# Attention outputs in two blocks of eight heads instead of four blocks of four, in a four-layer transformer kernel

## The reference, cut to what matters

```python
h = layernorm(x) * (1 + scale1) + shift1
q, k, v = h @ Wq + bq, h @ Wk + bk, h @ Wv + bv        # 16 heads of 16
p = softmax(q @ k.T * HEAD_DIM ** -0.5)                # per head, 256 x 256
x = x + gate1 * ((p @ v) @ Wo + bo)
h = layernorm(x) * (1 + scale2) + shift2
x = x + gate2 * (gelu(h @ W1 + b1) @ W2 + b2)          # blocks 0, 1, 3
# block 2 instead: h1 = attention + x;  x = layernorm(h1) * gamma + beta + h1
```

## Time and profile before

| what | us |
|---|---|
| median of 3 runs | 1201.23 (1201.06 to 1201.85) |
| profiled execution | 1202.65 |
| its span, first to last instruction | 1200.8 |
| busy in the span: PE, DVE, ACT, POOL | 1100.7, 806.5, 560.7, 173.5 |
| MLP steps of layer 0, from projection to projection | 36.5 to 37.7 |
| layer 2 steps, from projection to projection | 28.7 to 30.3, most of them |

### The profile page before, as it was taken

The page is one execution under the profiler, slowest core; times in us unless marked ns, Lnnn a source line. Parts: engine busy times, 40 slices in busy tenths (PEclk is TensorE's granted clock), DMA queues, the critical chain, the costliest instruction groups (busy, mean ns, idle before and its releaser), DMA issues.

```text
span 1200.8 us, 22222 instructions
## 1 busy us (share of the span) xinstructions
PE 1100.7 (92%) x7540; PEld 840.9 (70%) x7540; DVE 806.5 (67%) x2245; ACT 560.7 (47%) x1122; POOL 173.5 (14%) x288
## 2 busy tenths in 40 slices
PE   5799999999999999999999988888888999999996
PEld 4567777777777777777777665555555777777765
DVE  4576667666677667766577677777778666776642
ACT  4235554545643455444554434444444455554451
POOL 3010110101102211010110011111114101111010
PEclk9789999999999999999999999999999999999998
DMA  7542333123343233312333323333353133322300
GB/s 234 181 147 72 107 108 92 59 63 105 107 151 147 78 107 107 90 56 70 106 108 116 109 63 115 105 114 112 113 164 124 58 107 116 116 76 65 92 24 18
DMA packets 102714, 123.18 MB, mean 103 GB/s; under 512 B 8992, under 2 KB 96032, under 8 KB 101600
## 3 DMA queue, kind: packets, MB, share of 16 engines
q1 hardware_dynamic: 102048, 121.73, 32.6%
q10 hardware_dynamic: 576, 0.30, 0.1%
HBM read 85.16 MB, written 35.78 MB: 101 GB/s over the span
## 4 chain that ended last, share of the span: by engine, by line
PE 68%; DVE 13%; issue 6%; DMA 5%; ACT 4%; SPq 1%; ACTq 1%; DVEq 0%; POOL 0%; POOLq 0%
PE dense L1160 12%; PE dense L1091 9%; PE s_bank L1184 9%; PE o_bank L1239 8%; PE dense L1146 8%; PE st_bank L1221 6%; DMA q_stack<-max_t 4%; DVE neg_max L790 4%; PE o_bank L1120 3%; PE o_bank L1106 2%; PE o_bank L1070 2%; PE o_bank L1246 2%; PE s_bank L1194 2%; ACT xn L550 2%; DVE s_bank L785 1%
## 5 line engine op out<-in xcount | busy, mean ns | idle before, releaser
L602 ACT ACTIVATE probs<-st_bank 128x512 f32<-128x512 f32 (+1 forms) x512 | 263.8, 568 | 251.8 <-PE st_bank L1221 188.8
L790 DVE TENSOR_REDUCE neg_max<-s_bank 128x2 f32<-128x512 f32 x384 | 256.3, 684 | 70.0 <-PE s_bank L1184 66.1
L1184 PE MATMUL s_bank<-k_stack,q_stack 96*128 96x256 f32 (+1 forms) x1024 | 232.1, 318 | 18.8 <-DMA k_stack<-qk_dram 8.3
L1184 PEld LDWEIGHTS s_bank<-k_stack,q_stack 96*128 96x128 f32 x1024 | 166.1, 194 | 71.1 <-issue 24.5
L1160 PE MATMUL dense<-w_sb,hid 128*128 128x256 f32 x768 | 201.0, 380 | 0.0
L1221 PE MATMUL st_bank<-q_stack,k_stack 98*128 98x512 f32 x384 | 151.2, 467 | 7.7 <-DMA q_stack<-max_t 6.8
L443 POOL TENSOR_TENSOR veps<-mv,eps_c 128x2 f32<-128x2 f32 x65 | 12.7, 195 | 983.6 <-DVE mv L756 902.9
L1239 PE MATMUL o_bank<-probs,v_aug 128*32 128x256 f32 (+1 forms) x2048 | 132.2, 376 | 22.1 <-ACT v_aug L542 18.1
L1160 PEld LDWEIGHTS dense<-w_sb,hid 128*128 128x128 f32 x768 | 130.5, 189 | 10.6 <-issue 0.4
L1091 PE MATMUL dense<-ht,w_sb 128*128 128x256 f32 x512 | 127.4, 389 | 3.8 <-ACT ht L550 1.5
L590 ACT ACTIVATE hid<-dense,vec 128x256 f32<-128x256 f32 x192 | 80.5, 470 | 101.2 <-PE dense L1146 101.2
(11 more groups left out here) (122 smaller groups left out, 1489.9 us busy)
## 6 DMA issues: line engine op xcount, KB each, us to landing
q_stack<-qk_dram SPq DMA_DIRECT2D x192, 128.0 KB, 2.9
k_stack<-qk_dram SPq DMA_DIRECT2D x96, 256.0 KB, 4.1
par_sb<-par_dram SPq DMA_DIRECT2D x32, 512.0 KB, 5.5
qk_dram<-q_hi SPq DMA_DIRECT2D x32, 256.0 KB, 2.2
qk_dram<-q_lo SPq DMA_DIRECT2D x32, 256.0 KB, 2.2
qk_dram<-k_hi SPq DMA_DIRECT2D x32, 256.0 KB, 2.1
qk_dram<-k_lo SPq DMA_DIRECT2D x32, 256.0 KB, 2.1
w_sb<-w SPq DMA_DIRECT2D x3, 1280.0 KB, 9.2
```

The costliest lines, as they stand in the source:

```text
L602: nc.scalar.activation(probs[p % 4][:, kt, :, q0:N], src, ACT.Exp, scale=SCORE_SCALE[l]).then_inc(p_sb, 1)
L790: nc.vector.tensor_reduce(neg_max[:, qt, 2 * p:2 * p + 2], split3(bank[:]), AX.X, ALU.max, negate=True).then_inc(s_max, 1)
L1184: ins = mm(bank[:, e * N:e * N + k1], q_stack[g.par][0:KB, 2 * p + e, qt * P:(qt + 1) * P].bitcast(F32R), k_stack[g.par][0:KB, p, 0:k1].bi ...
```

## The change

`values`, `out_copy`, `out_turn` and `out_norm` are done twice a step for eight heads instead of four times for four. A block fills both output banks, its copy moves 512 columns, its reciprocal takes 16 numbers a row; the multiply stays at one instruction for four heads. In MLP steps the places of these blocks move: on PE `ht2_t` comes before the first block, and the first block after the first up product; in the second half of the step one block stands where most of the down products are done, and `ao_turn` moves to the end. On ACT `modulate2` comes one `exps` earlier. In the steps without MLP work `out_copy` moves from DVE to ACT. In layer 2 the second norm's multiplication by `rstd` is folded into the second residual, and the loop of layer 2 is written out.

```diff
@@ run_steps
-                first = B - 1 if CAUSAL[l] else 3
+                written_out = CAUSAL[l] or not HAS_MLP[l]
+                first = B - 1 if written_out else 3
@@ scalar
+            def out_copy(g, h):
+                wait(act, o_ps, g.count(2, h + 1))
+                wait(act, ot_ps, g.count(2, h))
+                nc.scalar.activation(o_sb[:], o_banks[:, :, 0:N], ACT.Copy).then_inc(o_copy, 1)
@@ exps
-                    if p % 2 == 0:
-                        wait(act, o_ps, g.count(4, p // 2 - 1) if p >= 4 else g.count(4, p // 2 + 3 - 4))
+                    if p % 4 == 0:
+                        wait(act, o_ps, g.count(2, p // 4))
@@ scalar step
-                exps(g, 2, 3)
+                exps(g, 2)
                 if mlp:
                     modulate2(c)
+                exps(g, 3)
...
                     max_rows(act, g, 1)
+                    out_copy(g, 0)
                 exps(g, 4, 5, 6, 7)
+                if not mlp:
+                    out_copy(g, 1)
@@ vector: layer 2's second norm and residual
-                    times_gate(c, xn2, 2, prod2)
+                    for t in range(T):
+                        ins = stt(x_of(c)[:, t], prod[:, t], rstd[:, 1, t:t + 1], xg[1][:, t], ALU.mult, ALU.add)
...
+                        ins = stt(prod[:, t], x1[:, t], mv[:, 1, t, 0:1], par_sb[c.par][:, 2], ALU.subtract, ALU.mult)
@@ vector step, MLP
+                    ht2_split(c)
+                    maxima(g, 12, 13, 14)
                     out_copy(g, 0)
-                    maxima(g, 12)
-                    ht2_split(c)
-                    maxima(g, 13)
-                    out_norm(g, 0)
-                    out_copy(g, 1)
-                    maxima(g, 14)
-                    out_norm(g, 1)
                     maxima(g, 15)
                     max_split(g, 1)
+                    out_norm(g, 0)
                     max_copy(g, 1)
...
+                        maxima(a, 5, 6)
+                    out_copy(g, 1)
+                        maxima(a, 7)
                         max_split(a, 0)
+                    out_norm(g, 1)
                         max_copy(a, 0)
@@ tensor step, MLP
                     score_t(g, 2)
-                    values(g, 0)
+                    ht2_t(c, a)
                     score(g, 12)
                     v_product(a, 0)
                     score_t(g, 3)
-                    ht2_t(c, a)
                     v_product(a, 1)
-                    out_turn(g, 0)
                     score(g, 13)
-                    values(g, 1)
                     mlp_up(c, a, 0, 0)
                     score(g, 14)
-                    out_turn(g, 1)
+                    values(g, 0)
                     mlp_up(c, a, 0, 1)
                     score(g, 15)
                     mlp_up(c, a, 1, 0)
+                    out_turn(g, 0)
                     mlp_up(c, a, 1, 1)
...
+                    # second half: score_t(g, 5..7) and score(a, 2..6) between down products, then
+                    mlp_down(c, 11, 12)
+                    values(g, 1)
+                    score(a, 7)
+                    mlp_down(c, 12, 14)
+                    out_turn(g, 1)
+                    mlp_down(c, 14, 15)
+                    max_turn(a, 0)
+                    mlp_down(c, 15, 16)
+                    ao_turn(g)
```

More of the change, by code:

```diff
@@ L870, in second_norm, with out_copy, out_norm @@
[L870 to L872 removed]
+            def out_copy(g, h):
+                wait(dve, o_ps, g.count(2, h + 1))
+                wait(dve, ot_ps, g.count(2, h))
+                nc.vector.tensor_copy(o_sb[:], o_banks[:, :, 0:N]).then_inc(o_copy, 1)
+            def out_norm(g, h):
+                wait(dve, ot_ps, g.count(2, h + 1))
+                o5 = o_banks[:, :, N:2 * N].rearrange("p i (t h d) -> p i t h d", t=T, h=4)
+                wait(dve, ao_sb, g.count(4, 2 * h))
+                nc.vector.reciprocal(rec[:], o5[:, :, :, :, HD]).then_inc(rec_sb, 1)
+                wait(dve, rec_sb, g.count(2, h + 1))
+                if h == 0:
+                    wait(dve, aot_ps, g.count(1, 0))
+                for i in range(2):
+                    c0 = 4 * HD * (2 * h + i)
+                    dst = ao[:, :, c0:c0 + 4 * HD].rearrange("p t (h d) -> p t h d", h=4)
+                    nc.vector.tensor_tensor(dst, o5[:, i, :, :, 0:HD],
+                                            rec[:, i].unsqueeze(3).to_broadcast([P, T, 4, HD]), ALU.mult).then_inc(ao_sb, 1)
@@ L873, in second_norm @@
+            def second_norm(c):
+                if c.layer == 2:
+                    wait(dve, ln2_mv, c.count(1, 1))
+                    stt = nc.vector.scalar_tensor_tensor
+                    for t in range(T):
+                        ins = stt(prod[:, t], x1[:, t], mv[:, 1, t, 0:1], par_sb[c.par][:, 2], ALU.subtract, ALU.mult)
+                    ins.then_inc(xn2_done, 1)
+                    return
+                wait(dve, w1_ps, c.mlp(4, 0))
                 normalize(c, x1, 1, ln2_rstd, xn2, xn2_done)
@@ L1221, in score_t @@
                         mm(split3(st_bank[kt][:]), *stacks(g, p, kt, 0), start=True, stop=True).then_inc(st_ps, 1)
[L1223 to L1233, removed]
-                wait(pe, p_sb, g.count(16, 4 * q + 4))
-                for kt in range(T):
-                    q0 = P if CAUSAL[g.layer] and kt else 0
-                    for j in range(4):
-                        pr = probs[(2 * q + j // 2) % 4]
-                        ins = mm(o_bank[q % 2][32 * j:32 * j + 32, q0:N], v_aug[g.par][:, kt, 4 * q + j, :],
-                                 pr[:, kt, j % 2, q0:N], start=kt == 0, stop=kt == T - 1)
-                ins.then_inc(o_ps, 1)
@@ L1243, in out_turn, with values @@
-            def out_turn(g, q):
-                wait(pe, o_copy, g.count(4, q + 1))
-                for t in range(T):
-                    ins = tr(o_bank[q % 2][:, N + t * P:N + (t + 1) * P], o_sb[q % 2][:, t * P:(t + 1) * P], ident[:])
+            def values(g, h):
+                if h == 0:
+                    wait(pe, v_sb, g.count(1, 2) if g.ahead(1).exists else g.count(1, 1))
+                    if g.off > 0:
+                        wait(pe, x1_done, g.count(1, 0))
+                else:
+                    wait(pe, ao_sb, g.count(4, 2))
+                wait(pe, p_sb, g.count(16, 8 * h + 8))
+                for i in range(2):
+                    for kt in range(T):
+                        q0 = P if CAUSAL[g.layer] and kt else 0
+                        for j in range(4):
+                            pr = probs[2 * i + j // 2]
+                            ins = mm(o_bank[i][32 * j:32 * j + 32, q0:N], v_aug[g.par][:, kt, 8 * h + 4 * i + j, :],
+                                     pr[:, kt, j % 2, q0:N], start=kt == 0, stop=kt == T - 1)
+                ins.then_inc(o_ps, 1)
@@ L1247, in out_turn @@
+            def out_turn(g, h):
+                wait(pe, o_copy, g.count(2, h + 1))
+                for i in range(2):
+                    for t in range(T):
+                        ins = tr(o_bank[i][:, N + t * P:N + (t + 1) * P], o_sb[:, i, t * P:(t + 1) * P], ident[:])
                 ins.then_inc(ot_ps, 1)
@@ L1354, in step @@
                     values(g, 0)
+                    score_t(g, 4)
                     out_turn(g, 0)
-                    values(g, 1)
-                    score_t(g, 4)
-                    out_turn(g, 1)
                     score(a, 0, 1)
```

88 lines of the change are left out of this document (29 added, 59 removed).

## The result

| | us | runs |
|---|---|---|
| before, run beside it | 1201.85 (1199.78 to 1205.14) | 7 |
| after | 1194.83 (1186.62 to 1197.26) | 7 |
| ratio | 0.9934, 95% interval 0.9914 to 0.9953 | |
| profiled execution of after, its span | 1196.37, 1194.6 | |

What follows compares the result with a forecast made beforehand. PE was taken to bound the 23 MLP steps, a chain across engines layer 2. 15 x -0.73 + 8 x -1.01 + 0 = -19.0 us from the profiled 1202.65 gave 1183.6, as median of the runs 1182; range 1171 to 1198.

Steps and rivals of the forecast that it cites:

- the layer 2 steps come to 0: Eight layer 2 steps: +0.8 us from a later DVE maximum and -0.8 from the written-out loop cancel.
- counted at -0.73 like the others: MLP steps of layers 0 and 3, the last included: each 0.73 us shorter.
- the first half: MLP step, projection to `score_t(4)`: -0.10 us in layers 0 and 3, -0.38 in layer 1.
- the second half: MLP step, `score_t(4)` to next projection: blocks -0.38, freed waits -0.65, new tail +0.4, together -0.63 us.
- The joint: PE's change into and out of four-heads-abreast mode: 0.31 us a block, bounds 0.2 and 0.4, two fewer a step.
- The wait on the norm: First half of MLP steps, PE before the moved `ht2_t`: +0.85 us in layers 0 and 3, +0.4 in layer 1.
- The second half's tail: MLP step, last block through copy, divide and `ao_turn` to projection at 6.3 us; PE waits 0.4, bounds 0 and 1.0.
- The slower rival: MLP steps: last block's chain through DVE and ACT longer than laid out; at a 1.6 us wait, 1210; chance 0.12.
- The rival of no change: MLP steps: `ht2_t` late by its full 1.1 us, none of the second half's 0.9 freed; near 1200; chance 0.08.
- the -0.8 for the loop: Layer 2: writing out the loop saves at most 0.47 us once and less in three more steps, -0.8 in all.
- the prediction's own last sign of being wrong: Changed trace, layer 2: the prediction is wrong if the half-clock stretches there become many.
- PE's clock falls in the layer 2 steps: Rival: two PE waits, before first block and `score_t(4)`, halve the clock in seven more steps; 11 us back, 1193; chance 0.10.

Runs made afterwards that it cites:

- e11_four_blocks: Kernel after, but layer 2 with four blocks of four heads in the old order, norm folded, loop written out, last MLP step as before: 1181.37 us, ratio 0.9816.
- e6_last_old: Kernel after, but all layer 2 steps and the last MLP step as before the change: 1182.97 us, ratio 0.9835.
- e3_last_ht2: Kernel after, with `ht2_t` behind `score_t(3)` again in the last MLP step only: 1195.21 us, ratio 0.9951.
- e1_fill: Kernel after, plus unread matmuls in layer 2 steps, five ahead of `values(0)`, three ahead of `score_t(4)`: 1194.37 us, ratio 0.9940.
- e5_sparse_fill: Kernel after, plus six unread matmuls per layer 2 step between `score_t(4)` and the second output block: 1190.67 us, ratio 0.9899.
- e9_norm_alone: Kernel after, but layer 2 and last MLP step as before, and POOL's `addend` waiting for DVE's second norm: 1179.21 us, ratio 0.9806.
- e7_ht2_later: Kernel after, but layer 2 steps as before and `ht2_t` behind the first v product in MLP steps: 1190.64 us, ratio 0.9901.
- e8_joint: Kernel after, but layer 2 steps as before and one small full-array matmul inside each MLP-step block of eight: 1193.55 us, ratio 0.9927.

## Why the prediction was right in its sign and wrong in its size

In short: the term that failed is "the layer 2 steps come to 0", with the clock left out of the sum. From the 16th to the 24th projection the time grew by 6.8 us where 1.0 less was forecast, with 27.3 us at half clock instead of 6.8. The second is the last MLP step, counted at -0.73 like the others, which grew by 5.5. The MLP steps, on which the sum rests, came out near the forecast or better.

**The MLP steps: right, with terms that made up for one another.** In layer 0 the first half (projection to `score_t(4)`) became 0.14 shorter on average over the first seven steps (forecast 0.10), the second half 0.89 (forecast 0.63); the eighth step, longer than the others, gave 2.3. Layer 1 gave 1.09 a step (forecast 1.01), layer 3 about 0.5 (forecast 0.73). By the scatter above these means are good to 0.2 or 0.3. The joint was sized at 0.31 a block and measured 0.1 to 0.2; that the sum came out all the same is in part luck. The wait on `v_aug` of the earlier trace rows is gone. The wait on the norm came as forecast: 8.6 us in the first 15 steps, 0.57 each, where the terms 0.85 and 0.4 average 0.64.

**The second half's tail: the chain was right, the wait was not.** The last block and what follows it, to lay beside the earlier trace rows:

```profile
254.17 1.93 PE L1252 MATMUL o_banks<-probs,v_aug 128*32 128x256 f32 x32
256.04 0.50 PE L1199 MATMUL s_bank<-k_stack,q_stack 96*128 96x256 f32 x2
256.18 0.69 DVE L874 COPY o_sb<-o_banks 128x512 f32<-128x512 f32 x1 [1.64 <-PE o_banks L1252]
...
257.97 0.26 DVE L881 RECIPROCAL rec<-o_banks 128x16 f32<-128x16 f32 x1
...
258.80 0.66 PE L1085 MATMUL o_banks<-ident,ao 128*128 128x128 f32 x4
...
259.50 0.84 ACT L583 ACTIVATE ao_t<-o_banks,vec 128x256 f32<-128x256 f32 x2 [6.14 <-PE o_banks L1085]
259.65 0.72 PE L1199 MATMUL s_bank<-k_stack,q_stack 96*128 96x256 f32 x4
...
260.48 1.96 PE L1135 MATMUL o_banks<-w_sb,ao_t 128*128 128x256 f32 x8
```

Copy at +2.0, divide at +3.8, `ao_turn` at +4.6, projection at +6.3 from the block: each as laid out. But PE's own work to the projection was 6.2 long, not 5.9 (two transpositions and the scores behind them), so the 0.4 us wait is hardly there (0.11 ahead of the projection at 260.48). The block's 1.87 from its start to the next engine work, and the copy's 0.7, were right too. The slower rival, that the tail decides, falls with this. The rival of no change writes -0.38 + 0.15 for its first half, where +0.15 is already the sum with the -0.38 in it; the time near 1200 that it gives stands.

**Layer 2: the step that failed.** "The layer 2 steps come to 0" held only at full clock: 28.65 us from the projection at 800.15 to the next, against 28.71. Its two parts were not as laid out either: the -0.8 for the loop is not there (steps of 28.9 to 29.0 us written out in `e11_four_blocks`, 28.94 on average with the loop in `e6_last_old`), while blocks of eight made the full-clock steps 0.1 to 0.2 shorter (after, `e3_last_ht2`) and not 0.1 longer. The many stretches at half clock are the prediction's own last sign of being wrong. The rival "PE's clock falls in the layer 2 steps" had the mechanism and nearly the time (1193), at a chance of 0.10. The time is partly luck, since about 8 of its 11 us came in layer 2 and the rest in the last MLP step; and its place was wrong: not the two waits (`e1_fill`), but the thin stretch that a block of eight leaves behind `score_t(4)` (`e5_sparse_fill`, `e11_four_blocks`). The Trainium skill (TensorE: Matmul & The Clock Gate, HAM oscillation — how this bites in real kernels) speaks of gaps in which PE is idle; ahead of the fall at 680.40 no wait in that step was over 0.83, so here the clock fell at a PE that was at work with pauses. What the clock wants is not shown by these runs: in the first layer 2 step of before it fell with PE at work all the time, on the small matmuls at 698.94. And the falls are not the same in two executions.

**The last MLP step: overlooked.** It was counted at -0.73 with the others. It has no q, k, v products, and without them PE comes early to the moved `ht2_t`:

```profile
1134.82 1.11 PE L1085 MATMUL dense<-ident,xn 128*128 128x128 f32 x4 [2.73 <-DVE xn L774]
```

2.73 us instead of 0.78 before, and the clock is at half from 1134.3 on. The wait alone is 1.95 more; the rest of the 5.45 came with 10.2 us at half clock. That the place of `ht2_t` is the whole cause is not shown (`e3_last_ht2` moved it and kept 6.8 at half clock); that the new order and blocks are, is (`e6_last_old`).

**At one clock the sum was near.** Over the runs, after has a granted clock of 0.971 where before has 0.978: 2 x 0.007 x 1195 = 17 us more at half clock, worth about 8 if PE sets the pace there. By this estimate the change gives -7 - 8 = -15, against -19 forecast. It is a rough one: the granted clock is that of the whole execution, and in layer 2 PE does not set the pace everywhere.

## What to carry to other kernels

A larger block is a longer wait for its inputs: before merging blocks, look in the timeline what PE does in the place that the merged block leaves, and take the edit only in the steps where other work fills it. Read the granted clock of every stretch with the time of a change, and check the steps that lack some of the work (the first, the last) one by one when an order is shared. A wait on a slow instruction is better mended at what makes that instruction slow (`e9_norm_alone`, some 0.3 us a step) than by moving its reader (`e7_ht2_later`, nothing).

## What the runs showed of the hardware that was not expected

- The granted clock fell to 0.50 in steps where PE was busy for all but short waits (2.24 to 2.39 of the 3.0 us ahead of the four falls of after), and in different steps from one execution to the next (after, `e3_last_ht2`): the seven runs of after lie between 1186.62 at a mean granted clock of 0.978 and 1197.26 at 0.969.
- It also fell, in the first layer 2 step of eleven of the 14 traces, while 32 small matmuls ran that keep PE at work without a pause (3.73 us in before), or up to 0.6 us behind them.
- A change between four heads side by side and the full array and back cost PE 0.1 to 0.2 us (`e8_joint`), the small matmul that made it counted in.
- Two instructions of DVE that take 0.73 us (`e9_norm_alone`) took 1.74 beside one addition of POOL (after).
